# Constants and the second group's mask loaded as transfers of their own, the big weights last, and every engine's order drawn anew

## The reference, cut to what matters

```python
# layer L0: latents = x, keys and values from [ctx, x]; 16 heads of 16 channels
h = concatenate([ctx, x], axis=1)                      # 128 tokens per item
q = latents @ q_w + q_b;  k, v = split(h @ kv_w + kv_b)
attn = softmax(where(mask, q k^T / 16, -inf))          # the mask is over the 64 ctx tokens
a = attn v @ out_w + out_b + residual
o = rmsnorm(a) * postnorm_w
x = gelu(o @ mlp_w1 + mlp_b1) @ mlp_w2 + mlp_b2 + residual      # 256 -> 1024 -> 256
# layer L1: input = x, context = ctx, seen as (64 channels, 256 positions); 8 heads
xn = (x - mean) * rsqrt(var) * gamma + beta            # over an item
q = Wq xn;  k, v = Wkv ctx
y = softmax(q^T k * scale) v                           # 256 x 256 for each head
out = x + Wo y + bo
```

## Time and profile before

| | |
|---|---|
| median of 3 runs | 602.03 us (601.12, 602.03, 604.49) |
| the profiled execution's own time | 603.94 us |
| its span in the trace | 602.0 us |
| TensorE matmul busy | 570.4 us |
| VectorE busy | 547.9 us |
| ScalarE, GpSimd busy | 504.4 us, 420.8 us |
| granted clock of TensorE, mean | 0.983 of full |

### The profile page before, as it was taken

The page is one execution under the profiler, slowest core; times in us unless marked ns, Lnnn a source line. Parts: engine busy times, 40 slices in busy tenths (PEclk is TensorE's granted clock), DMA queues, the critical chain, the costliest instruction groups (busy, mean ns, idle before and its releaser), DMA issues.

```text
span 602.0 us, 21122 instructions
## 1 busy us (share of the span) xinstructions
PE 570.4 (95%) x8564; PEld 463.7 (77%) x8564; DVE 547.9 (91%) x1053; ACT 504.4 (84%) x1904; POOL 420.8 (70%) x419
## 2 busy tenths in 40 slices
PE   4799999999999999999999999999999999998976
PEld 4689877777888787887888777887877777876755
DVE  5977889999999999999899989998999999999996
ACT  2848779988899987998899888998989897968873
POOL 2643468777588767796777865886676985787764
PEclk9779999999999999999999999999999999999989
DMA  8213001011102111111111111011111111110110
GB/s 285 76 38 103 22 19 55 20 37 30 35 29 57 43 38 28 38 56 32 33 46 55 38 38 27 31 35 29 37 29 38 32 38 40 37 29 20 40 24 23
DMA packets 50080, 26.45 MB, mean 44 GB/s; under 512 B 38048, under 2 KB 48320, under 8 KB 49984
## 3 DMA queue, kind: packets, MB, share of 16 engines
q1 hardware_dynamic: 49984, 25.11, 15.3%
HBM read 22.99 MB, written 2.10 MB: 42 GB/s over the span
## 4 chain that ended last, share of the span: by engine, by line
PE 64%; DVE 23%; ACT 6%; POOL 4%; DMA 2%; issue 1%; SPq 0%
PE bank L671 60%; DVE E1b L1179 6%; DVE nm L1162 5%; PE bank L792 4%; POOL E1b L1445 3%; ACT E1b L1362 3%; DVE nm L1017 2%; DVE E L1027 2%; DMA mski<-in_msk 1%; DVE QS L1155 1%; ACT E L1259 1%; DVE PT L1035 1%; DVE hm L1099 1%; ACT hm L1333 1%; DVE mrow L989 1%; PE bank L822 1%
## 5 line engine op out<-in xcount | busy, mean ns | idle before, releaser
L1445 POOL TENSOR_TENSOR E1b<-E1b,rs 128x512 f32<-128x512 f32 x255 | 264.0, 1060 | 85.4 <-DVE rs L1168 80.4
L1362 ACT ACTIVATE E1b<-bank,nm 128x256 f32<-128x256 f32 x512 | 237.0, 495 | 28.6 <-DVE nm L1162 28.4
L1162 DVE TENSOR_REDUCE nm<-bank 128x2 f32<-128x512 f32 x256 | 164.2, 674 | 9.4 <-PE bank L671 9.0
L1179 DVE STREAM_TRANSPOSE E1b<-E1b 128x1024 f32<-128x1024 f32 x128 | 155.9, 1227 | 5.7 <-POOL E1b L1445 4.8
L671 PE MATMUL bank<-ctx,QS 64*128 64x256 f32 x1024 | 134.5, 394 | 1.7 <-DVE PT L1035 1.0
L671 PE MATMUL bank<-E1b,CT 32*64 32x256 f32 (+1 forms) x4224 | 120.9, 375 | 10.2 <-ACT E1b L1362 3.6
L671 PEld LDWEIGHTS bank<-E1b,CT 32*64 32x64 f32 x4224 | 95.4, 132 | 30.4 <-ACT E1b L1362 5.1
L1362 ACT ACTIVATION_READ_ACCUMULATOR E1b<-bank,nm 128x1 f32 x512 | 116.7, 228 | 0.0
L671 PEld LDWEIGHTS bank<-ctx,QS 64*128 64x128 f32 x1024 | 91.6, 186 | 25.5 <-issue 6.8
L1259 ACT ACTIVATE E<-bank,nm 128x128 f32<-128x128 f32 x256 | 90.7, 409 | 9.6 <-DVE nm L1017 9.6
L1259 ACT ACTIVATION_READ_ACCUMULATOR E<-bank,nm 128x1 f32 x256 | 63.8, 249 | 0.0
(11 more groups left out here) (119 smaller groups left out, 823.1 us busy)
## 6 DMA issues: line engine op xcount, KB each, us to landing
CT<-in_hT SPq DMA_DIRECT2D x256, 32.0 KB, 1.9
hraw<-in_hT SPq DMA_DIRECT2D x8, 512.0 KB, 3.4
ctx<-in_ctx SPq DMA_DIRECT2D x32, 128.0 KB, 2.7
xnat<-in_xn SPq DMA_DIRECT2D x8, 256.0 KB, 2.8
E1b<-in_w SPq DMA_DIRECT2D x2, 1024.0 KB, 8.8
out<-y SPq DMA_DIRECT2D x16, 128.0 KB, 1.7
E1b<-in_kvw SPq DMA_DIRECT2D x2, 256.0 KB, 4.6
mski<-in_msk SPq DMA_DIRECT2D x32, 1.0 KB
```

Of the source, the lines that this page charges most:

```text
L1162: e.tensor_reduce(nm1[:, u % 16, :], bank[place["S", u]][:, :].rearrange("p (i t) -> p i t", i=2), AX.X, ALU.max, negate=True).then_inc(dv ...
L1179: e.transpose(E1b[:, k:k + 2, :, :], E1b[:, k:k + 2, :, :]).then_inc(dve_steps, 1)
L1362: t = e.activation(E1b[:, r, i, :], bank[bk][:, i * 256:(i + 1) * 256], ACT.Exp, bias=nm1[:, r, i:i + 1], scale=1.0, accum_out=sum1[:, r, ...
L1445: e.tensor_tensor(E1b[:, u % 16, :, :], E1b[:, u % 16, :, :], rs1[:, u % 16, :].unsqueeze(2).to_broadcast([128, 2, 256]), ALU.mult).then_i ...
```

## The change

The small constants come in two transfers. `sm0` brings columns 0 to 46 (47 x 4 bytes x 128 partitions = 24 KB: biases, scales, the head masks and the exponents `mh`), `sm1` the other 768 columns (`ob`, `b2`, `ident`, `avg`) on a semaphore of its own, for which the first `t`, `obtd`, `avg` and `xop` now wait. The step `lh` is cut in two: `lh` loads a group's tokens as soon as the tokens before are split, `lm` its mask once the mask before is used. At the start SP now issues in the order tokens, key weight, first constants, query weight, value weight, mask, output weight, other constants, `lx`; then tokens and mask of group 1; then `w10`, `w20`, `l10`, which wait for `mk` of group 0 instead of `hlo` of group 0 and stand behind `lm` of group 1 in the plan. Before, the second MLP weight was issued first, ahead of tokens and mask of group 1, and the other two behind them.

The constants of the planner and all its `SHIFT` entries are new. No arithmetic is added or removed, and no step but `sm1` and `lm`.

```diff
--- before.py
+++ after.py
-WIN = (-48.4, 20.6)
-HEADAT = -484
-PREP = 16
-LATE = (-2, -12.75, 11, -4.25, 0.25, -1.75, 5.5, 8.75)
-STAY = dict(full=0, rows=0.6, grid=2, cols=1.5, rows32=1.5, cols32=0)
-PREFER = (0, 2)
+WIN = (-48.4, 22.5)
+HEADAT = -74
+PREP = 17
+LATE = (-1, 0.5, 2.5, 11.5, -7, -15.75, 10, 10.75)
+STAY = dict(full=2, rows=0.3, grid=0.3, cols=1.5, rows32=2, cols32=4)
+PREFER = (0, 6)
...
-    34.5, "Qe.0": 4.75, "Qe.1": -1.25, "Qe0": -4.25, "S": 1, "S.0": -0.25, "S.2": -1.5, "S.4": 0.25, "S.6":
...
-    "V.1": 11.25, "V0": 22.25, "Ve": 1.75, "Ve.0": -15.5, "Ve.1": -11.75, "Ve0": 2, "W1": 12.25, "W1.0": -7,
...
-    "X.4": 4.5, "X.5": -31.25, "X.6": 40, "X.7": 21.25, "X0": -5.5, "X1": 1.75, "X1.0": -0.5, "X1.1": -8,
-    "X1.2": -15.25, "X1.3": 20.5, "X1.4": -6.25, "X1.5": 1.75, "X1.6": -14, "X1.7": 9, "X10": 25, "Y": -33.5,
...
-    "sn.1": -6.25, "sn.2": 2, "sn.3": -3.25, "sn0": -33.5, "snp": 3.5, "snp.0": 13.75, "snp.1": -2, "snp.2":
-    -5.25, "snp.3": -23.75, "snp0": -20, "sq": 10.25, "sq.0": 6, "sq.1": -10.5, "sq.2": -9.25, "sq.3": -4.5,
...
-    "var.5": -6, "var.6": 1, "var.7": 10.5, "var0": 0.75, "w10": -1, "w1h": 11.75, "w1h.0": 1.5, "w1h.1": 1.25,
-    "w1h.2": 7.25, "w1h.3": 40, "w1h0": -30.25, "w1l": 33.25, "w1l.0": -10.75, "w1l.1": -7.75, "w1l.2": -1.5,
...
+    "S": 0.25, "S.0": 0.75, "S.2": 0.25, "S.4": 1, "S.6": -2.75, "S0": -4.25, "U": 32.5, "U.0": -8, "U.2": 19,
...
+    "Ve.1": -4.75, "Ve0": -17, "W1": 15.25, "W1.0": -38.25, "W1.1": -27.5, "W1.2": -2.5, "W1.3": -4, "W10":
...
+    "X1": 6.25, "X1.0": 1, "X1.1": 8, "X1.2": -0.5, "X1.3": -9.5, "X1.4": 38, "X1.5": 1.5, "X1.6": -18.75,
+    "X1.7": 8, "X10": -10.5, "Y": -39.25, "Y.0": -11.75, "Y.1": -4.25, "Y.2": 39.5, "Y.4": -14.75, "Y.5": -1.5,
...
+    -18, "sn0": 2.75, "snp": -4, "snp.0": -0.25, "snp.1": -0.75, "snp.2": 1, "snp.3": -0.25, "snp0": -21.25,
...
+    "var.7": 9.25, "var0": 12, "w10": -13.75, "w1h": 35.5, "w1h.0": 25.25, "w1h.1": -3.25, "w1h.2": -11.5,
+    "w1h.3": -18.5, "w1h0": 2.75, "w1l": 38.75, "w1l.0": 16.75, "w1l.1": -5.25, "w1l.2": -11.75, "w1l.3": 8,
...
 SM = dict(qb=(0, 2), kb=(2, 2), vb=(4, 2), b1=(6, 8), pw=(14, 2), gamma=(16, 1), beta=(17, 1),
-          bo=(18, 1), bq=(19, 8), bv=(27, 8), par=(35, 2), hm=(37, 8), ob=(45, 256), b2=(301, 256),
-          ident=(557, 128), avg=(685, 128), mh=(813, 2))
+          bo=(18, 1), bq=(19, 8), bv=(27, 8), par=(35, 2), hm=(37, 8), mh=(45, 2), ob=(47, 256), b2=(303, 256),
+          ident=(559, 128), avg=(687, 128))
+SMA = 47
 SMW = 815
...
-    "w20": (700, 13000), "l10": (700, 14500), "lh": (1700, 5500), "out": (500, 2200),
+    "w20": (700, 13000), "l10": (700, 14500), "lh": (480, 4000), "lm": (1250, 3500), "sm1": (450, 6000), "out": (500, 2200),
...
-    for k, name in enumerate(("h0", "wk0", "wq0", "wv0", "sm0", "m0", "wo0", "lx")):
-        add(name, *((0,) if name == "lx" else ()), on=D, at=-2000 + k)
+    for k, name in enumerate(("h0", "wk0", "sm0", "wq0", "wv0", "m0", "wo0", "sm1", "lx")):
+        add(name, *((0,) if name == "lx" else ()), on=D, at=-20000 + 200 * k)
     for k, name in enumerate(("w10", "w20", "l10")):
-        add(name, on=D, at=-900 + k, after=[("hlo", 0)])
+        add(name, on=D, at=-10000 + 200 * k, after=[("lm", 1)])
     for k, x in enumerate("kqvo"):
...
         if g:
-            add("lh", g, on=D, at=at() if g > 1 else -1000, after=[("hlo", g - 1), ("mk", g - 1)])
+            add("lh", g, on=D, at=at() if g > 1 else -12000, after=[("hlo", g - 1)])
+            add("lm", g, on=D, at=at() if g > 1 else -11000, after=[("mk", g - 1)])
         add("hhi", g, on=A + P, at=at(), after=[("lh", g) if g else ("h0",)] + (
             [(n, g - 1, i) for n in "KV" for i in range(2)] + [("Q", g - 1)] if g else []))
         add("hlo", g, on=G + A, at=at(), after=[("hhi", g)])
-        add("mk", g, on=A, at=at(), after=[("lh", g) if g else ("m0",)] + (
+        add("mk", g, on=A, at=at(), after=[("lm", g) if g else ("m0",)] + (
...
-                add("t", g, c, r, on=V, at=at(0.4), after=[("snp", g, c, r), prev("o", p1)], banks=[("t", g, c, r)], kind="other")
+                add("t", g, c, r, on=V, at=at(0.4), after=[("snp", g, c, r), prev("o", p1), ("sm1",)], banks=[("t", g, c, r)], kind="other")
...
-        add("xop", g, on=G, at=at(), after=[("lx", g), ("obtd",), ("sm0",), ("y", g - 1) if g else None])
+        add("xop", g, on=G, at=at(), after=[("lx", g), ("obtd",), ("sm1",), ("y", g - 1) if g else None])
...
-    add("obtd", on=A, at=HEADAT + 8, after=[("obt",)], empties=(("obt",), "other"))
+    add("obtd", on=A, at=HEADAT + 8, after=[("obt",), ("sm1",)], empties=(("obt",), "other"))
...
-        add("avg", p, on=V, at=at, after=[("bn", p), ("sm0",)], banks=[("avg", p)], kind="other")
+        add("avg", p, on=V, at=at, after=[("bn", p), ("sm1",)], banks=[("avg", p)], kind="other")
...
                 elif name == "sm0":
-                    e.dma_start(small[:, :], sm_d).then_inc(d_sm, 16)
+                    e.dma_start(small[:, 0:SMA], sm_d[:, 0:SMA]).then_inc(d_sm, 16)
+                elif name == "sm1":
+                    e.dma_start(small[:, SMA:SMW], sm_d[:, SMA:SMW]).then_inc(d_s2, 16)
                 elif name == "m0":
                     w.wait_ge(pool_init, 1)
                     load_mask(0)
                 elif name == "wo0":
                     e.dma_start(sto[:, :, :], ow_d.rearrange("(k p) n -> p k n", p=128)).then_inc(d_o, 16)
                 elif name == "w10":
-                    w.wait_ge(*done("hlo", 0))
+                    w.wait_ge(*done("mk", 0))
                     e.dma_start(stw1[:, :, :], w1_d.rearrange("(k p) n -> p k n", p=128)).then_inc(d_w1, 16)
                 elif name == "w20":
-                    w.wait_ge(*done("hlo", 0))
+                    w.wait_ge(*done("mk", 0))
                     e.dma_start(stage[:, :, :], w2_d.rearrange("(k p) n -> p k n", p=128)).then_inc(d_w2, 16)
                 elif name == "l10":
-                    w.wait_ge(*done("hlo", 0))
+                    w.wait_ge(*done("mk", 0))
                     e.dma_start(l1w[:, :, :], l1_d.rearrange("w o n -> o w n")).then_inc(d_l1, 16)
                 elif name == "lh":
                     g, = key
                     w.wait_ge(*done("hlo", g - 1))
                     load_h(g)
+                elif name == "lm":
+                    g, = key
                     w.wait_ge(*done("mk", g - 1))
                     load_mask(g)
                 elif name == "lx":
...
                 elif name == "t":
                     g, c, r = key
+                    w.wait_ge(d_s2, 16)
                     w.wait_ge(*done("snp", g, c, r))
...
                     w.wait_ge(*done("bn", p))
-                    w.wait_ge(d_sm, 16)
+                    w.wait_ge(d_s2, 16)
                     mm(pb[:, 0:1], sm("avg"), mv[:, 0:1], True, True).then_inc(pe_steps, 1)
```

More of the change, by code:

```diff
@@ L542, in build @@
         place, steps = pl.place, pl.steps
-        d_sm, d_q, d_k, d_v, d_o, d_w1, d_w2, d_l1, d_mk, d_h, d_x = (
-            sem(n) for n in ("d_sm", "d_q", "d_k", "d_v", "d_o", "d_w1", "d_w2", "d_l1", "d_mk", "d_h", "d_x"))
+        d_sm, d_s2, d_q, d_k, d_v, d_o, d_w1, d_w2, d_l1, d_mk, d_h, d_x = (
+            sem(n) for n in ("d_sm", "d_s2", "d_q", "d_k", "d_v", "d_o", "d_w1", "d_w2", "d_l1", "d_mk", "d_h", "d_x"))
         d_out, d_ct = ([sem(f"{n}{i}") for i in range(2)] for n in ("d_out", "d_ct"))
```

## The result

| | before | after |
|---|---|---|
| median, 5 runs each | 602.03 us (601.12 to 604.49) | 612.83 us (610.49 to 613.15) |
| profiled execution, its span | 603.94, 602.0 us | 613.08, 611.1 us |

The changed kernel takes 1.0165 times as long, 95% interval [1.0138, 1.0191]: 10 us slower, where 598.2 us and at most 605.5 were forecast. In the changed kernel the lines have moved: L1162 is L1171, L1117 is L1126, L792 is L800, L1027 is L1035, L1023 is L1031, L961 is L969, L955 is L963.

The account below looks back on a forecast made before the run. TensorE was taken to bound the kernel (busy 570.4 of 602.0 us), with VectorE bounding the end; start and mask -1.65, middle -1.0 and end -1.2 gave -3.85 us, so 598.2 us, range 592 to 605.5.

Parts of the forecast that it names:

- The order at the start: Group 0's softmax: weight splits now stand behind it instead of delaying it; -1.25 us, bounds 0 and -3.2.
- The loads: Start: VectorE's 1.33 us wait for group 1's mask goes, gaining 0.4 us; split constants and other load moves count 0.
- The things named to be seen: Profile signs at the start: no L955 between `smax` and the second `snp`, second L792 near 21 us instead of 22.59.
- The rival of the late splits: Start: weight splits put off over 9.7 us delay group 0's `W1` to `X1`; 606 us, chance 0.18 including a worse draw.
- The clock: TensorE's low clock from 22 to 39 us: a pause stays, so 0, bounds 0 and -7.2.
- The middle: New constants, same policy redrawn: four more junctions of `S` pairs, -1.0 us, bounds -5.2 and +5.2; idle time 0.
- the rival of the order that gives the gain back: Middle: more bank waits or shorter `S` stretches cost +2 to +5 us; 601.5 us, chance 0.26 including nothing gained.
- The end: After the last `X1`: L0 ends five units later, so fewer L1 units in VectorE's stretch; -1.2 us, bounds -4 and +3.
- The signs of being wrong: Wrong if the clock holds, TensorE's idle time from 80 to 540 us moves over 4 us, or the first L1162 comes later.

Follow-up runs that it names:

- the like move in the old order: Old order with the new loads, second scaling (`snp`) of group 0's softmax put ahead of `w1h` 0, `w2h` 3 and `w2h` 2: 603.65 us against 602.84, 1.0016.
- the base: The kernel before with the new loads alone, all compute orders and PSUM banks as before: 602.65 us against 603.39, ratio 0.9991.
- the kernel with the cut at 461 us: New loads, order of the kernel before up to `X1` of group 6, near 461 us, the changed kernel's order from there: 610.70 us, 1.0136.
- the kernel with the old start (cut at the first `W1`): New loads, order of the kernel before up to group 0's first `W1`, the changed kernel's order from there: 609.0 us, 1.0109.

## Why the prediction was wrong

The step that failed is the one headed **The order at the start**: it counted a gain of 1.25 us, with bounds 0 and -3.2, for weight splits that go behind the softmax, and looked at the first half of the softmax alone. The runs show a loss of 4.2 us up to the first `W1` in its place, and some 4 us more up to 124 us. The work put off is done sooner or later in the same 20 us, on engines that had little room.

- *The loads*: 0.4 us forecast, 0.9991 [0.9970, 1.0012] measured, too wide to tell 0.4 us from nothing. The mechanism is seen: the wait of VectorE for the mask near 15 us is gone, and with the new loads and the old start the first `smax` begins 1.1 us after the first `s` where it began 1.5 us after it. The Trainium skill ("DMA: Bandwidth & Descriptors", Rules for kernel authors) speaks against small transfers; the measured ratio bears out no loss here that could be told.
- *The start*. The things named to be seen came: no L963 between `smax` and the second `snp`, the second L800 at 21.33 us (near 21 forecast). They were worth nothing: the like move in the old order gave 1.0016. With what it does besides, the new order costs 4.2 us up to the first `W1`. Moving three `w1l`, `Me` and one `w2l` behind the reciprocals of the second half took back 2.5 and 2.1 us of the whole in two kernels, so this part of the cause is shown; the rest of the start is not taken apart.
- *The rival of the late splits* had the right sign and nearly the size of the start's loss, 606, but not the mechanism. The last L969 starts at 40.1 us, sooner than the 41.7 of before, and `W1` does not wait for it. The splits hurt where they were done, not by when they were finished.
- *The clock* was taken as 0 with no bound on the side of a loss. Up to the first `X1` its mean is 0.91, where it was 0.88 before; but in the five traces with the old order up to there it was 0.88 three times and 0.93 twice, so this tells nothing, and TensorE's pauses have taken the place. And it falls again at 96 us, after pauses of TensorE of 1.45, 0.68 and 1.10 us in a row, and stays at 0.50 until 104. The `S` there, 16 matmuls, take 3.79 us where two pairs took 2.00. In the kernel with the old loads, where the same order has a mean clock of 0.97 in this stage and not 0.93, the stage is 0.9 us shorter: most of the 1.3 us that it is longer than in the base. The Trainium skill ("TensorE: Matmul & The Clock Gate", Part 1) lets the clock return soon after TensorE is kept busy; here it was still 0.50 after the 8 us from 38 to 46.
- *The middle*. Three stretches of `S` fewer (84 against 87) were forecast as four, worth -1.0 us. The term was sized about rightly: in the kernels with the new order from 124 or from 333 us, with 85 stretches, the 1024 matmuls of `S` took 134.0 us where they took 134.5 before. In the changed kernel they took 135.3, since those near 98 us ran at half clock. Against that stands the rival of the order that gives the gain back, +2 to +5 us: the middle is 2.2 us longer, all of it lost up to 333 us, but only part of it is new waiting: from 124 to 333 us TensorE idles for 1.8 us more and is busy for 0.8 us more with nearly the same work.
- *The end*. The forecast had the last `X1` five units later, worth -1.2 us. It did not move: 38 maxima (L1171) begin behind it, and 38 (L1162) did before; the 39 of the earlier trace rows count one from the 0.9 us ahead of the last `X1`. Due values five units apart made no difference to the order there. The stage is 0.25 us longer than in the base; in the nine traces with the new end it takes 70.9 to 72.4 us, in the five with the old one 70.4 to 71.3, so a loss nearer 1 us is what the traces together show.
- *The signs of being wrong*. One came: the first maximum starts at 93.0 us where it started at 87.3. TensorE's idle time from 80 to 540 us went from 8.25 to 10.69 us, by less than the 4 us that were named.

Of the loss between 51 and 124 us the engines of `sq` and `gs` and the low clock are known as causes within the stage from 79 us on; what is lost from 51 to 79 us stays open. So does which waits make the 2.2 us up to 333 us: in the changed kernel TensorE waits there six times, 2.3 us in all, for VectorE's `ZS` (L1194), and the base shows no such wait on `ZS` there, but no run took them away. No version ran that beats the kernel before.

## What to carry to other kernels

Where one list scheduler fills every engine, putting work off is not a gain: find the slot into which it falls, and who waits there, before counting what it frees. A kernel whose TensorE is at 99% for two thirds of its span carries each us lost at the start to its end, so price the start first, and to both sides. When all the tuning constants are new, treat the new order as a new draw, with a loss bound as wide as the gain bound, for the clock too. And read an experiment that changes several places stage by stage: a total that stays the same can hide a gain in one stage and a loss in another, as with the engines of the GELU sums.

## What the runs showed of the hardware

A pause can cost more than its length. In the kernel with the cut at 461 us one pause of 4.12 us was followed by some 5 us at a clock of 0.50 with TensorE busy, and the two stages beside it took 5.7 us longer than in the base.

Some of VectorE's instructions last longer beside GpSimd's. In the kernel with the old start (cut at the first `W1`):

```profile
85.41 0.67 DVE L1285 CUSTOM_DVE_ANT_0 AO<-xo 128x256 f32<-128x256 f32 x1
85.76 2.54 POOL L1622 TENSOR_TENSOR hh<-hraw,hh 128x1024 fp32r<-128x1024 f32 x1
...
86.01 2.57 DVE L1285 CUSTOM_DVE_ANT_0 AO<-xo 128x256 f32<-128x256 f32 x1
```

The same instruction takes 0.67 and then 2.57 us, the second time until GpSimd's 2.54 us are over. The `w1l` of 33.22 us shows it too, 2.31 us for two where the least is 0.472 each, beside a GpSimd instruction of 1.45 us. Not all do. In the kernel with the cut at 461 us three maxima, which read a PSUM bank, take 1.86 us together beside two GpSimd instructions, 0.62 each:

```profile
469.13 2.05 POOL L1645 TENSOR_TENSOR E1b<-E1b,rs 128x512 f32<-128x512 f32 x2
...
469.19 1.86 DVE L1215 TENSOR_REDUCE nm<-bank 128x4 f32<-128x512 f32 x3
```

That GpSimd's instructions cause the longer times is read from the overlap; no run took it apart.
